# A one-core transformer stack: side work of the first part's scan placed anew on VectorE, GpSimd and ScalarE

## The reference

```python
x = x + _L0_attn_ref(_layernorm(x), ln1_g, ln1_b, in_proj_w, conv_w, ..., ffn_b2)
...
def _mamba(x, ...):                      # inside: x + _mamba(_layer_norm(x)), then x + ffn(_layer_norm(x))
    xi, z = split(x @ in_proj_w)         # 256 channels each
    xc = silu(causal_conv(xi, 4 taps) + conv_b)
    dt, Bm, Cm = split(xc @ x_proj_w)    # rank 8, and 16 + 16 states
    dt = softplus(dt @ dt_proj_w + dt_proj_b)
    # for every token t, channel d, state n:
    h = exp(dt[t,d] * A[d,n]) * h + dt[t,d] * Bm[t,n] * xc[t,d]
    y[t,d] = sum_n h * Cm[t,n]
    return ((y + D * xc) * silu(z)) @ out_proj_w
```

## Time and profile before

| | us |
|---|---|
| three runs | 1402.18, 1400.39, 1397.42 |
| their median | 1400.39 |
| the profiled execution | 1401.11 |
| its span in the trace | 1399.4 |
| projections of the first part, in the span | 0 to 66 |
| its 64 units | 66.4 to 307.2 |
| the rest (feed-forward, routing, experts, three more layers) | 307.2 to 1399.4 |

### The profile page before, as it was taken

The page is one execution under the profiler, slowest core; times in us unless marked ns, Lnnn a source line. Parts: engine busy times, 40 slices in busy tenths (PEclk is TensorE's granted clock), DMA queues, the critical chain, the costliest instruction groups (busy, mean ns, idle before and its releaser), DMA issues. The chain is left out here.

```text
span 1399.4 us, 25149 instructions
## 1 busy us (share of the span) xinstructions
PE 1105.9 (79%) x8340; PEld 714.4 (51%) x8349; DVE 892.5 (64%) x2981; ACT 680.1 (49%) x1256; POOL 573.1 (41%) x739
## 2 busy tenths in 40 slices
PE   8876777679278644299936999859995999899998
PEld 3322222227178633199934777634333777654545
DVE  3599899995545456377549888743858778850200
ACT  2685466545134301132216888627664888641221
POOL 6188889882734414544435434120013655110000
PEclk9989999999589955599968999979996999999999
DMA  2999000000522215311120000020002000000000
GB/s 61 161 191 167 0 0 1 0 0 9 182 61 58 69 38 206 70 42 46 33 72 1 2 3 3 2 57 1 1 0 85 3 3 2 3 1 0 15 0 15
DMA packets 80456, 58.31 MB, mean 42 GB/s; under 512 B 14043, under 2 KB 69221, under 8 KB 80326
## 3 DMA queue, kind: packets, MB, share of 16 engines
q1 hardware_dynamic: 74630, 45.20, 15.3%
q0 software_dynamic: 4544, 9.38, 1.8%
q10 hardware_dynamic: 1152, 2.10, 0.4%
HBM read 28.13 MB, written 28.52 MB: 40 GB/s over the span
## 5 line engine op out<-in xcount | busy, mean ns | idle before, releaser
L713 PE MATMUL bank<-hC,ident 128*128 128x512 f32 x256 | 132.7, 643 | 48.7 <-POOL hC L998 46.7
L998 POOL TENSOR_TENSOR hC<-h,Cs 128x1024 f32<-128x1024 f32 x64 | 150.8, 2356 | 49.8 <-DVE h L897 49.5
L897 DVE TENSOR_TENSOR_SCAN h<-bank,state,dBx 128x512 f32<-128x512 f32 x128 | 157.3, 1270 | 3.7 <-POOL dBx L991 1.7
L1381 POOL DMA_INDIRECT moe_answers<-moe_yw,moe_xg x78 | 84.3, 1081 | 128.6 <-DVE moe_yw L1558 69.7
L2549 DVE CUSTOM_DVE_ANT_0 decay_below<-bank,decay_q_mask 128x256 bf16<-128x256 f32 x256 | 97.2, 419 | 23.0 <-PE bank L2361 22.1
L713 PEld LDWEIGHTS bank<-hC,ident 128*128 128x128 f32 x256 | 46.0, 197 | 111.2 <-POOL hC L998 71.8
L2549 DVE CUSTOM_DVE_ANT_0 window_below<-bank,window_q_mask 128x192 bf16<-128x192 f32 x256 | 80.4, 353 | 29.5 <-PE bank L2361 27.9
L810 ACT ACTIVATE bank<-dt,A 128x512 f32<-128x512 f32 x128 | 83.2, 683 | 28.1 <-DVE h L897 27.1
L1452 PE MATMUL bank<-moe_xgT,moe_wac 128*128 128x128 f32 x624 | 87.4, 286 | 6.5 <-issue 4.1
L2489 ACT ACTIVATE decay_pb<-bank 128x512 f32<-128x512 f32 x128 | 76.2, 598 | 33.3 <-PE bank L2376 32.7
L1467 PE MATMUL bank<-moe_wd,moe_hT 128*128 x624 | 83.0, 277 | 5.7 <-DVE moe_hT L1545 2.7
(11 more groups left out here) (480 smaller groups left out, 2834.2 us busy)
## 6 DMA issues: line engine op xcount, KB each, us to landing
moe_slots<-blank SPq DMA_DIRECT2D x16, 1040.0 KB, 17.6
moe_xg<-moe_slots SPq DMA_DIRECT2D x78, 65.0 KB, 1.9
moe_wa<-in_moe_w SPq DMA_DIRECT2D x2, 2048.0 KB, 9.5
moe_back<-moe_answers SPq DMA_DIRECT2D x8, 256.0 KB, 5.6
moe_back<-moe_answers ACTq DMA_DIRECT2D x8, 256.0 KB, 5.7
moe_wu<-in_moe_wu SPq DMA_DIRECT2D x1, 2048.0 KB
deep_w<-in_deep_w SPq DMA_DIRECT2D x3, 512.0 KB
moe_answers<-moe_yw,moe_xg POOLq DMA_INDIRECT x78, 2.5
```

Of the source, the lines that this page charges most:

```text
L713: last = nc.tensor.matmul(sum_bank(hh)[:], k.ident[:], hC[:, u % 2, hh, :], start=(n == 0), stop=(n == NS - 1))
L897: v.tensor_tensor_scan(h[:, u % 2, hh, :], decay_bank(u, hh)[:], dBx[:, u % 2, hh, :], state[:, n, hh:hh + 1], ALU.mult, ALU.add).then_inc ...
L998: g.tensor_tensor(hC[:, u % 2], h[:, u % 2], Cs[:, u % 2, None, :].to_broadcast([P, H, CW]), ALU.mult).then_inc(q_hC, 1)
L1381: nc.gpsimd.indirect_dma_start(answers, bass.IndirectOffsetOnAxis(index, 0), yw[:, i % NY, :], None)\
```

## The change

It changes only where side work stands in the scan of `mamba`:

- `residual(c - 1)` moves behind the scans of units 19, 35 and 51.
- `last_rest` for chunks 2 and 3 goes from VectorE (units 15 and 16) to GpSimd, behind the `hC` and the shared dBx of units 18 and 19; `take_low` goes from units 18 and 19 to 20 and 21.
- `xo` and the bias of chunks 2 and 3 go from GpSimd's scan queue to its projection queue, with a semaphore of their own.
- dBx is shared from unit 20 on, where it was 24.

```diff
-    WD, FIRST_SHARED = 384, 24
+    WD, FIRST_SHARED = 384, 20
...
@@ project_gpsimd
             g.iota(k.blank[:, :, P].bitcast(U32), pattern=[[P, 2 * k.E]], base=2 * k.N, channel_multiplier=1)\
                 .then_inc(k.made_blank, 1)
+            pool.wait_ge(s_rs, 3)
+            for c in range(2, C):
+                for n in range(c * CT, (c + 1) * CT):
+                    last = g.tensor_scalar(xo[:, n, :], k.X[:, n, :], k.meanvar[:, n, 0:1], k.rstd[:, n:n + 1],
+                                           ALU.subtract, ALU.mult)
+                last.then_inc(s_xop, 1)
             add_bias(1)
+            pool.wait_ge(s_xn, C)
+            for c in range(2, C):
+                pool.wait_ge(s_xop, c - 1)
+                xt = k.X[:, tiles_of(c), :]
+                g.tensor_tensor(xt, xt, w2b[:, None, :].to_broadcast([P, CT, P]), ALU.add).then_inc(s_xb, 1)
@@ scan_scalar
-                if u in (18, 19):
-                    take_low(u - 16)
+                if u in (20, 21):
+                    take_low(u - 18)
@@ scan_vector
-                if u in (15, 16):
-                    last_rest(u - 13)
                 if c and n == 1:
                     gated(c - 1)
-                if c and n == 3:
-                    residual(c - 1)
...
                     v.tensor_tensor_scan(h[:, u % 2, hh, :], decay_bank(u, hh)[:], dBx[:, u % 2, hh, :],
                                          state[:, n, hh:hh + 1], ALU.mult, ALU.add).then_inc(q_h, 1)
+                if c and n == 3:
+                    residual(c - 1)
@@ scan_gpsimd
+            def last_rest(c):
+                pool.wait_ge(s_mid, c + 1)
+                pool.wait_ge(s_lo, c - 1)
+                pool.wait_ge(q_hC, c + 17)
+                pool.wait_ge(q_rest, shared(c + 19))
+                g.tensor_tensor(rt2[96:128, c % 2, :], rt1[96:128, c % 2, :], BC3[96:128, cols(c)], ALU.subtract)\
+                    .then_inc(s_r2, 1)
+                pool.wait_ge(s_r2, c + 1)
...
-                if u in (18, 22):
-                    outer_norm(2 + (u - 18) // 4)
-                if u in (20, 24):
-                    add_bias(2 + (u - 20) // 4)
+                if u in (18, 19):
+                    last_rest(u - 16)
```

## The result

| | before | after |
|---|---|---|
| median of five runs | 1400.63 | 1390.18 |
| lowest, highest | 1397.42, 1402.18 | 1389.88, 1393.07 |
| the profiled execution | 1401.11 | 1391.92 |
| its span | 1399.4 | 1390.2 |
| first dBx | 66.44 | 66.55 |

All in us. The ratio of the runs is 0.993, 95% interval 0.9919 to 0.9941. The change saves 10.45 us by the medians, 9.2 by the profiled executions; the prediction said 13.0. In the trace the saving is 9.72 us, all of it in the scan; 0.1 and 0.4 us are lost ahead of it and behind it.

The account below looks back on a forecast made before the run. VectorE was taken to set the scan's pace, through its side work and idle time. The terms 3.74 + (7.45 - 4.19) - 1.04 + 2.78 + 4.22 summed to 12.96 us saved, giving a median of 1387.4; range 1383 to 1393.5.

Parts of the forecast that it names:

- the likeliest case: Whole kernel: the forecast itself holds, median between 1386 and 1389.5 us; chance 0.55.
- the longer chain: Rival, first boundary: slow TensorE clock and slower subtraction cost 3.7 us, giving 1391.1; chance 0.17 shared with another rival.
- units 15 and 16: Scan: both subtractions leave VectorE, so the two units become bare, saving 3.74 us.
- unit 19: First boundary: residual behind the scans hides its wait given a fast sum; unit falls from 7.45 to 4.19 us.
- units 20 to 23: Scan: earlier sharing saves 1.06 us but a chain adds waits of 0.6 and 1.5; 1.04 lost.
- units 24 to 27: Scan: normalisation and bias gone from GpSimd's queue, 16.54 us becomes 13.76, saving 2.78.
- units 35 and 51: Later boundaries: residual's 2.11 us wait hidden behind the scans in each, together 4.22 saved.
- The work moved into the projections: Before the scan: 8.9 us more on GpSimd fits its idle time; nothing charged, at most 8.9.
- The boundary chain: Units 20 to 23: share, GpSimd subtraction, low part, C copy, decays, B copy in sequence; VectorE loses 0.6 and 1.5 us.
- the clock at the boundaries: Sum over unit 17 on TensorE: expected fast, 1.98 us instead of 3.58; slow clock would cost 0.86.
- the moved subtraction holds VectorE up: Rival, scan: GpSimd's subtraction locks out VectorE, costing 3.68 us, giving 1391.1; chance 0.17 shared with another rival.
- The clock behind the scan: Rival, behind 307 us: lower TensorE clock turns the gain into a loss, 1405.3 us at grant 0.78; chance 0.05.

Follow-up runs that it names:

- x6: Kernel after with the two subtractions back on VectorE in units 15 and 16, low parts in 18 and 19: scan 230.83 us, median 1392.7.
- x1: Kernel after with the subtractions behind hC of units 17 and 18, ahead of the shares of dBx: scan 227.90 us, median 1388.33.
- x2: Kernel after with dBx shared from unit 24 again instead of 20: scan 228.13 us, median 1388.28.
- x3: Kernel after with C's row spread four times in a chunk's last two and first four units: scan 228.04 us, median 1388.99.
- x5: Kernel before with only normalisation and bias of chunks 2 and 3 moved into the projections: scan 238.30 us, median 1399.04.
- x9: Kernel after with the subtractions on VectorE between the two scans of units 17 and 18: scan 228.81 us, one run 1392.04.
- x7: Kernel after with subtractions ahead of the shares and C's row spread four times at chunk boundaries, together: scan 225.72 us, median 1386.93.
- x10: Kernel after with subtractions ahead of shares, C's row spread four times at boundaries, dBx shared from unit 18: scan 226.18 us, median 1387.29.

## Why the prediction was right, and where 3 us went

The forecast direction and its mechanisms hold, and 1390.18 lies in the stated range; the likeliest case, 1386 to 1389.5, was missed by 0.7 us. The range held because it reached to the rivals near 1391, and one of these, the longer chain, came in part. The profiled execution, 1391.92 against 1388.15 forecast, shows the miss better than the median does. Step by step, measured on the profiled executions:

| step | predicted | measured |
|---|---|---|
| units 15 and 16 | 3.74 saved | 3.74 |
| unit 19 | 3.26 saved | 2.40 |
| units 20 to 23 | 1.04 lost | 2.12 lost |
| units 24 to 27 | 2.78 saved | 2.93 |
| units 35 and 51 | 4.22 saved | 2.09 + 0.70 |
| sum in the scan | 12.96 | 9.72 (0.02 lost elsewhere) |

**The work moved into the projections** cost nothing, as charged: the eight xo end at 47.0, the biases at 53.7, and the first dBx is 0.1 us later. One of them did run beside VectorE's subtraction, at 44.07 us, which by the prediction would make that 1.84 us long; it stayed at 0.69.

**Units 15 to 18** are right to 0.1 us, and x6 shows the other side.

**The boundary chain** is shown: the place of the subtraction behind the share (x1 takes the waits away), sharing (x2 does, too), and the sequence low part, C's copy, decays, B's copy. The subtraction took 1.15 us on GpSimd with 0.17 ahead of it, for which I had put 1.26 between bounds of 0.69 and 1.84. With the fast clock (x3) the two waits are 0.67 and 1.48, where I had worked out 0.6 and 1.5.

**The step that failed is the clock at the boundaries.** I wrote that with bare units ahead of unit 17 I expected the fast 1.98, since I had put the slow sum down to the stretched units 15 and 16. That step is refuted: the kernel after has bare units and a sum of 3.03 us. The price was right, since the 0.86 that I had given for a slow clock there is what unit 19 lost. Stretched units do go with a low clock: in the three kernels with the subtraction between dBx and scans of units 15 and 16 (before, x5, x6) the sum of unit 15 or 16 or both took 3.44 to 3.78 us, and in the other nine none of them did. But they don't tell where it falls, and bare units don't keep it away. The clearest pair is x2 and the kernel after. Up to the sum of unit 17 every engine has the same instructions in the same order, and VectorE's starts agree to 0.01 us from the first dBx on; only that first dBx stands at 66.14 us in x2 and at 66.55 in the kernel after. TensorE of x2_share_24, the sum of unit 15, that of unit 17 and the projection, where the kernel after has 1.96, 3.03 and 2.62 with the same idle times:

```profile
130.10 1.96 PE L724 MATMUL bank<-hC,ident 128*128 128x512 f32 x4 [0.81 <-POOL hC L1005]
...
134.68 1.98 PE L724 MATMUL bank<-hC,ident 128*128 128x512 f32 x4 [0.71 <-POOL hC L1005]
136.50 1.95 PE L739 MATMUL bank<-outw,yT 128*128 128x128 f32 x16
```

What decides it in one place and not in the other stays open. I had given unit 51 the gain of unit 35 by repetition, and had no term for the clock there. The terms for unit 19 (0.86), for units 20 to 23 (1.08, of which the later B row is 0.8 by x3) and for unit 51 (1.4) less the 0.15 that units 24 to 27 gave more, are the whole difference of 3.2. Of the 27 boundaries of the nine kernels without extra matmuls before the sum, 13 had a slow sum there (2.85 to 3.68 us), one or two in each kernel; in x9 one of them is hidden, since its longer units 17 and 18 give the projection time. In the three kernels with the extra matmuls none of 9 had.

**The rivals.** The longer chain (1391.1 if all its parts came) is what happened in its first part, with 0.86 and about 0.8 of the 3.7. That the moved subtraction holds VectorE up is refuted: no scan or dBx beside it is longer (1270 and 1196 ns). The Trainium skill's sentence in "Perfetto Trace Analysis", that a move between these two engines "might not help", is thus not borne out for the ports here. It came out so all the same for the move as made: in x6, with the work left on VectorE, the scan is as short as in the kernel after. But the reason is the place in the queue, not the ports; in x1's place the same move is worth 2.9 us of scan against x6. Units 36 and 37 had no new waits.

**The clock behind the scan** was my slower rival. It did not come: from 400 to 800 us the granted clock is 0.83 on the mean before and after, with TensorE busy for 279 us in both. The rest moved by 0.4 us between before and after; over the twelve profiled kernels it lies between 1090.6 and 1094.6 without order. A part of it shows right behind the scan: VectorE waits for the last projection 4.78 us in eight kernels and 6.3 to 6.5 in the other four (x1, x2, x6, x9), and these four alone have the low clock in that stretch (x1: granted 0.50 from 302.4 to 305.7 us). Against a spread of that size, the 2.2 to 2.3 us between the scans of x1 and x3 and that of x7 can't be read from the runs, let alone the 0.5 between x7 and x10. What sets it in each kernel stays open.

## What to carry to other kernels

When a step moves to an idle engine, look at what its new neighbour in the queue waits for: the same two subtractions cost 3 us behind a share that waited for another engine, and nothing ahead of it (x1). When two edits meet on one chain, price them in each other's company: the residual's move gained nothing at the first boundary and 2.1 us at the second. And where TensorE waits between its matmuls ahead of a sum that others wait for, take its duration at the lower clock level as a case with a real chance, even where the trace shows it fast.

## What the runs showed of the hardware

- The same fp32 sum of four matmuls took 1.98 us or 2.9 to 3.7, and the projection behind it 1.95 or up to 2.8. With the same instructions ahead of it on every engine and the same idle time on TensorE just before it, it took 1.98 in x2 and 3.03 in the kernel after. With three more short matmuls per unit right before it, some 0.2 us each, it stayed at 2.4 GHz at all 9 boundaries (x3, x7, x10).
- VectorE's subtraction with two SBUF inputs took 1.84 us when begun early in GpSimd's two-input multiplication, and GpSimd's next two-input instruction then took 1.71 instead of 1.27 (before, units 15 and 16). Between two of them it took 0.69. Begun 0.29 us before the end of one of GpSimd's one-input normalisations in the projections it stayed at 0.69, at 44.07 us in the kernel after, and it was GpSimd's next one that was longer: 785 ns in the median of the eight, 1068 for that one.
- A GpSimd instruction on 32 of the 128 partitions took 1.15 us where one on all 128 with the same 512 elements per partition took 1.27 (1.15 in the kernel after, 1.27 in the kernel before): a quarter of the partitions saved a tenth of the time.
